# Four style-modulated convolutions as one: two start-up products move from VectorE to ScalarE, and two small pieces of work change places

## The reference

```python
for i, typ in enumerate(('same', 'upsample', 'same', 'downsample')):
    s = style @ mw[i].T + mb[i]                      # a scale per sample and input channel
    weight = SCALE * w[i] * s[:, None, :, None]
    demod = rsqrt(sum(weight * weight, axis=(2, 3)) + EPS)
    weight = weight * demod[:, :, None, None]        # 64 x 64 x 3, one per sample
    out = conv(out, weight) + b[i][None, :, None]    # 'upsample' and 'downsample' also blur with 1 3 3 1
return x + out
```

## Time and profile before

| | |
|---|---|
| median of 3 runs | 649.97 us (649.73 to 650.28) |
| the profiled execution | 650.42 us, its span 648.6 us |
| PE busy | 639.6 us, 99% of the span |
| DVE busy | 538.3 us, 83% |
| ACT, POOL busy | 387.0 and 388.9 us, 60% each |
| granted PE clock | 1.0 of full speed throughout |
| transfers | 125.05 MB, 193 GB/s on average |

### The profile page before, as it was taken

How to read it: one execution, slowest core, us unless ns; L and a number is a source line. 1 busy time by engine, 2 the same in 40 slices (tenths; PEclk the granted TensorE clock), 3 DMA queues, 4 the chain that set the end, 5 groups by cost and what they waited for, 6 DMA issues and landing times.

```text
span 648.6 us, 13049 instructions
## 1 busy us (share of the span) xinstructions
PE 639.6 (99%) x4756; PEld 613.6 (95%) x4756; DVE 538.3 (83%) x682; ACT 387.0 (60%) x752; POOL 388.9 (60%) x358
## 2 busy tenths in 40 slices
PE   9999999999999999999999999999999999999997
PEld 7799899999999999999999999999999999999987
DVE  5987988999898777789998987777989897787873
ACT  4776455765655766655766655666555666655552
POOL 3257477766566766467765666765657766557630
PEclk9999999999999999999999999999999999999999
DMA  8129888679877877986778878768977768987784
GB/s 264 38 72 255 212 189 205 158 199 228 208 169 193 207 205 200 222 202 158 184 198 219 206 180 215 193 180 209 232 169 191 186 185 220 225 211 179 182 202 162
DMA packets 145855, 125.05 MB, mean 193 GB/s; under 512 B 6080, under 2 KB 112512, under 8 KB 145792
## 3 DMA queue, kind: packets, MB, share of 16 engines
q1 hardware_dynamic: 145424, 123.97, 76.5%
q10 hardware_dynamic: 368, 0.25, 0.1%
HBM read 36.51 MB, written 33.75 MB: 108 GB/s over the span
## 4 chain that ended last, share of the span: by engine, by line
PE 90%; DVE 5%; ACT 2%; issue 1%; POOL 1%; DVEq 0%; ACTq 0%; POOLq 0%
PE po L203 14%; PE po L204 14%; PE po L205 14%; PE pg L203 8%; PE pg L205 8%; PE pg L204 8%; PE pm L205 5%; PE pm L204 5%; PE pm L203 5%; PE pg L208 4%; PE pg L209 4%; PE pe L460 1%; PE pg L469 1%; DVE T L868 1%; DVE W L920 0%
## 5 line engine op out<-in xcount | busy, mean ns | idle before, releaser
L203 PE MATMUL po<-xh,W 128*128 128x256 f32 (+1 forms) x640 | 199.9, 312 | 1.6 <-DVE T L868 1.2
L204 PE MATMUL po<-xl,W 128*128 128x256 f32 (+1 forms) x640 | 199.5, 312 | 0.0
L205 PE MATMUL po<-xh,W 128*128 128x256 f32 (+1 forms) x640 | 198.7, 311 | 0.0
L203 PEld LDWEIGHTS po<-xh,W 128*128 128x128 f32 x640 | 125.2, 196 | 7.4 <-issue 2.1
L205 PEld LDWEIGHTS po<-xh,W 128*128 128x128 f32 x640 | 125.4, 196 | 5.8
L204 PEld LDWEIGHTS po<-xl,W 128*128 128x128 f32 x640 | 126.0, 197 | 5.0
L859 DVE TENSOR_TENSOR xl<-X,xh 128x1290 fp32r<-128x1290 f32 (+1 forms) x64 | 126.3, 1974 | 4.9 <-ACT xh L573 3.9
L634 ACT CAST Gh<-Gf 128x512 fp32r<-128x512 f32 x64 | 39.5, 620 | 123.6 <-DVE Gf L890 123.6
L573 ACT CAST xh<-X 128x1290 fp32r<-128x1290 f32 (+1 forms) x64 | 87.6, 1369 | 18.3 <-PE po L205 14.7
L868 DVE SCALAR_TENSOR_TENSOR T<-po,DD,M 128x512 f32<-128x512 f32 x96 | 71.3, 743 | 31.3 <-ACT M L580 21.2
L580 ACT ACTIVATE M<-pm,cv,DD 128x256 f32<-128x256 f32 x96 | 54.0, 563 | 66.8 <-PE pm L205 65.8
(11 more groups left out here) (179 smaller groups left out, 1734.9 us busy)
## 6 DMA issues: line engine op xcount, KB each, us to landing
X<-in_xin SPq DMA_DIRECT2D x64, 516.0 KB, 4.5
out<-T SPq DMA_DIRECT2D x63, 512.0 KB, 5.8
W<-W SPq DMA_DIRECT2D x90, 256.0 KB, 4.3
W<-W SPq DMA_DIRECT2D x30, 384.0 KB, 5.6
V<-V SPq DMA_DIRECT2D x32, 256.0 KB, 5.0
V<-W SPq DMA_DIRECT2D x32, 128.0 KB, 4.4
V<-Vx SPq DMA_DIRECT2D x32, 128.0 KB, 4.0
W<-W SPq DMA_DIRECT2D x9, 128.0 KB, 3.0
```

The lines of the kernel that those rows point to most:

```text
L203: eng.matmul(o, wh_, rh, start=first, stop=False)
L204: eng.matmul(o, wh_, rl, start=False, stop=False)
L205: return eng.matmul(o, wl_, rh, start=False, stop=last)
```

## The change

1. tmp[:, 0] and tmp[:, 1] are made by two ACT activations (Copy, with the bias as scale), which wait for D10c and stand in ACT's queue in front of `high(0, 2)`; DVE's two instructions go. The factor 2 of the second moves into DVE's later update of tmp[:, 1], which becomes a scalar_tensor_tensor in the place of a tensor_tensor and waits for ACT's second product. PE's small matmul on tmp[:, 0] waits for ACT in the place of DVE.
2. The three products of `edges_begin` are made in the place of sample 4, in front of `x_low(3)`; `edge_in(0)`, which was their tail, stays in the place of sample 5.
3. In group NGR - 2 = 30, place 2 (sample 122), ACT makes `sums_high(31)`, the copies V and Vx of the last group's sums, ahead of `m_out(122)` and not behind it.

```diff
@@ -189,7 +189,7 @@
         s_wxh, s_wxl, s_x0h, s_x0l = sem("wxh"), sem("wxl"), sem("x0h"), sem("x0l")
 
 
-        SC_S, SC_SQ2, SC_A2, SC_S1, SC_D32, SC_A, SC_D10, SC_K1, SC_D, SC_K2, SC_K3, SC_CV = range(1, 13)
+        SC_S, SC_SQ2, SC_A2, SC_S1, SC_D32, SC_A, SC_D10, SC_D, SC_K2, SC_K3, SC_CV = range(1, 12)
 
         K_A2, K_B1, K_C, K_B1D = 1, 2, 3, 4
         def bc(ap, n):
@@ -541,7 +541,7 @@
             for x in PROLOGUE[7:]:
                 unit(*x)
             pe.wait_ge(s_in["ed"], 16)
-            pe.wait_ge(s_sc, SC_K1)
+            pe.wait_ge(s_ss, 4)
             for t in range(3):
                 m = pe.matmul(pe_[0:64, 0:128], E[0:64, 1, t, 0:64], tmp[0:64, 0, :], start=t == 0, stop=t == 2)
             m.then_inc(s_pp, 1)
@@ -673,6 +673,9 @@
             act.copy(B1dh[:], pb[1].rearrange("p (i h) o -> p i h o", h=2)).then_inc(s_k0, 1)
             q3_full(1)
             q3_high(1)
+            act.wait_ge(s_sc, SC_D10)
+            act.activation(tmp[:, 0], DD[:, 1], ACT.Copy, scale=BB[:, 0, 0:1]).then_inc(s_ss, 1)
+            act.activation(tmp[:, 1], S[:, P2], ACT.Copy, scale=BB[:, 0, 1:2]).then_inc(s_ss, 1)
             high(0, 2)
             high(0, 3)
             act.wait_ge(s_x[0], 16)
@@ -732,9 +735,9 @@
                         x_high(2 * g + 2)
                 elif i == 2:
                     highs(b, (4, 6))
-                    m_out(b)
                     if g == NGR - 2:
                         sums_behind(b - 1)
+                    m_out(b)
                     if g in (0, NGR - 2):
                         x_high(2 * g + 2)
                     sums_behind(b)
@@ -989,9 +992,6 @@
                 link(tt(b0z[:], AA[:, 0], DD[:, 0], ALU.mult))
                 tt(D10[:], DD[:, 0], DD[:, 1], ALU.mult)
                 link(dve.tensor_scalar(b0z[:], b0z[:], bias(0), None, ALU.mult))
-                dve.wait_ge(s_in["xe"], 16)
-                dve.wait_ge(s_ms, 2)
-                edge_in(0)
 
             def newton(l, t, step):
 
@@ -1056,8 +1056,6 @@
             reached(dve.scalar_tensor_tensor(out=D10c[:], in0=DD[:, 0], scalar=1.0 / 32.0, in1=DD[:, 1],
                                              op0=ALU.mult, op1=ALU.mult))
             dve.wait_ge(s_sc, SC_D10)
-            reached(dve.tensor_scalar(tmp[:, 0], DD[:, 1], bias(0), None, ALU.mult))
-            dve.tensor_scalar(tmp[:, 1], S[:, P2], bias(1), 2.0, ALU.mult, ALU.mult)
             full(0, 2)
             full(0, 3)
             g_low(0)
@@ -1074,7 +1072,9 @@
             sums(0)
             dve.wait_ge(s_pp, 5)
             link(tt(kt[lo], pe_[0:64, 0:128], D21[lo], ALU.mult))
-            reached(tt(tmp[lo, 1], tmp[lo, 1], kt[lo], ALU.add))
+            dve.wait_ge(s_ss, 5)
+            reached(dve.scalar_tensor_tensor(out=tmp[lo, 1], in0=tmp[lo, 1], scalar=2.0, in1=kt[lo],
+                                             op0=ALU.mult, op1=ALU.add))
             full(1, 0)
             full(1, 1)
             sums_low(0)
@@ -1103,12 +1103,16 @@
                     sums_low(weights_at(b - 1))
                 if i == 2 and g + 1 < NGR:
                     x_low(2 * g + 2)
+                if b == 4:
+                    edges_begin()
                 if b == 1:
                     x_low(1)
                 elif i == 0 and b:
                     x_low(2 * g + 1)
                 if b == 5:
-                    edges_begin()
+                    dve.wait_ge(s_in["xe"], 16)
+                    dve.wait_ge(s_ms, 2)
+                    edge_in(0)
                 for part, back in ((0, 1), (1, 2), (2, 6)):
                     if divmod(b - back, NG) in edge_at:
                         edge(*edge_at[divmod(b - back, NG)], part)
```

## The result

The changed kernel takes **647.17 us** (median of 5 runs, 646.56 to 647.62) against 649.97 (649.73 to 650.54): 2.80 us less, ratio 0.9955, 95% interval 0.994 to 0.997. The forecast was 647.0. The profiled execution took 647.62 us with a span of 645.8, against 650.42 and 648.6: also 2.8 less. So the two traces may be laid side by side, start by start.

What follows compares the result with a forecast made beforehand. PE, busy 99% of the span, was taken as the bound, so only its waits could pay: 0.35 + 0.66 + 1.05 + 0.40 + 0.2 + 3 x 0.1 = 2.96 us off 649.97 gave 647.0, range 646.3 to 648.8.

Steps and rivals of the forecast that it cites:

- the chain keeps most of it: Start-up, unit 4 to sample 0: most of Gl's 0.35 us gain lasts, ACT's copies being only 0.2 to 0.35 ahead.
- the lower bound: Start-up: only 0.2 us is gained if ACT's row of copies decides.
- the cover: Sample 4's place: DVE idled 2.53 us ahead of xl(3), so three products there delay nothing that PE shows.
- slow case: Sample 4's place: each product waits for a POOL instruction to end, all three done by about 58.25, xl(3) 0.1 later.
- rival a: Sample 4's place: products hold POOL up by 0.87 us, PE stands 0.6 us near 58, 647.6 us; chance 0.10.
- rival d: Sample 4's place: products delay POOL and with it PE's G product, so the kernel gets slower; chance 0.03.
- the gain: PE's waits for XS at the edges' first product, 0.66 us, and for T at sample 8, 1.05 of 1.14, go.
- slow restart: After a PE wait the second matmul also starts late, about 0.1 us, counted for three waits that go.
- rival c: Later groups: the wait returns at a group's first sample, taking back up to 2.0 us, 649.0 us; chance 0.15.
- rival b: Before sample 8: Vf, V low and xl(4) all blocked, T(6) 0.5 to 0.6 later, 647.6 us; chance 0.17.
- 0.40 + 0.2: Kernel's end: PE's wait before sample 123, 0.40 us, goes, and 0.2 of the 0.25 before sample 124.
- The rule about the shared ports: DVE instructions with two SBUF inputs contend with GpSimd's reads; whoever issues first keeps the ports for the whole instruction.

Runs made afterwards that it cites:

- e1: Kernel before with only the two constants' products moved to ACT: 650.02 us against 650.27, ratio 0.9995.
- e2: Kernel before with only the edges' three products moved to sample 4's place: 648.27 us against 650.27, ratio 0.9969.
- e3: Kernel before with only the last sums' copies put ahead of sample 122's M: 649.36 us against 650.27, ratio 0.9989.
- e5: Changed kernel with the edges' three products back in sample 5's place, but behind XS: 649.19 us, ratio 0.998 to the kernel before.
- e9: Changed kernel with the edges' three products made twice over in sample 4's place: 647.67 us, ratio 0.9963 to the kernel before.
- e6: Changed kernel with the edges' three products made three times over in sample 4's place: 648.17 us, ratio 0.9967 to the kernel before.
- e10: Changed kernel with the sums' copies ahead of M in the third place of every group, not only group 30: 646.29 us.

## Why the prediction was right, point by point

- **Part 1.** Forecast 0.35 us at Gl, bounds 0.2 to 0.4 at sample 0. Measured (changed kernel and e1): 0.38 and 0.37 at unit 4, 0.29 and 0.30 at sample 0. The step "the chain keeps most of it" lost 0.07 to 0.09, by the mechanism of the lower bound: ACT's copy of W (from 25.97) ends at 26.80 in both executions, so with the chance of 0.20 it gained 0.20 only, and DVE's low part of W behind it starts at 26.83, against 26.92 before, when DVE's own queue decided. The two ACT products cost nothing; they are issued 0.31 apart and overlap.
- **Part 2, the cover.** Forecast: slow case, products done at 58.25, xl(3) 0.1 later, nothing at PE. Measured: 58.17, 0.13, nothing. POOL was not held up (rival a): its two low parts took 0.79 and 0.74 us, against 0.74 and 0.73 before, and PE's products with G at 58 did not wait (rival d). POOL's room there is less than the 0.3 us that rival (a) counts, as a release takes 0.14 of it.
- **Part 2, the gain.** Forecast 0.66 + 1.05 and 0.1 for each slow restart, 1.91. Measured 1.88 at sample 8 and 2.00 to 2.02 at sample 9 (e2, and 2.11 - 0.09 in the changed kernel). The term that was off is T(6): forecast 73.8 on the time axis of the kernel before, measured 73.47 + 0.09 = 73.56. Vf lost only 0.24 (1.19 against 0.95) and not 0.6. XS lost 0.53 where 0.5 was forecast, but that is luck: the prediction had one of POOL's subtractions beside it, and it was Q3's low part, which had stood beside the first product before.
- **Given back (rival c), DVE not caught up (rival b).** e2 keeps its 1.9 us from sample 9 to the end. Both fall.
- **Part 3.** Forecast 0.40 + 0.2 + 0.1, bounds 0.4 to 0.8. Measured 0.79 and 0.78 (the changed kernel and e3). What the forecast lacked is the slow second matmul at sample 124 (0.09): it counts three such restarts in all, and there are four. M was not late: it starts at 625.58, and before at 627.58, with PE 2.00 ahead. The room for it, forecast as 0.6, does not hold if Vf is late: e5 shows that case.
- **The sum.** 2.96 forecast; by the ledger 0.29 (sample 0) + 0.67 (the edges' product) + 1.35 (sample 8 and the slow restarts, up to sample 9) + 0.79 (the end) = 3.10, less 0.20 of chance at start-up and 0.11 between samples 9 and 122, 2.79 in the profiled pair, and 2.80 in the medians. The forecast sum was thus 0.14 too small: 0.06 too much in part 1, 0.11 too little in part 2 and 0.09 in part 3, which partly cancel. That it agrees with the medians to 0.2 us is partly luck, since one comparison's medians can't tell 0.3 us (e1).
- **The rule about the shared ports** (the Trainium skill, page "SBUF — State Buffer", section "Who interferes with whom") has both its sides in these traces. With POOL first, DVE's products waited (1.20 us for one of 0.29). With DVE's xl first, POOL waited (2.32 us in e9). In e6 both lost: xl(3) waited for the POOL instruction in front of it, and POOL's next one waited for xl(3).

## What to carry to other kernels

When one engine is busy to 99%, list its waits one by one and price each as a difference of starts, the slow restart included; then a change to the work around it is worth what it removes from that list, and no more: the same reordering was worth 0.8 us in each of two places and nothing in 28 others, though it took some 22 us off VectorE's busy time there. Moving work into another engine's or place's idle time only pays if the queue behind it has room too: one place sooner gave 2.0 us, two places gave none, and three more products in the good place already cost 0.5 us through POOL, though VectorE itself had the time. Two waits in a row can be one: removing the first alone (e5) only moved its time into the second.

## What the runs showed of the hardware that was not expected

- A PE wait of 1.92 us was followed by 1.1 us of matmuls at the full clock and then, from 61.36 to 64.77, by matmuls 0.21 apart at the lower level (granted 0.83, 0.50 and 0.81 in three stretches of 2 us). Four of the twelve executions of that kernel, this one among them, have a mean clock of 0.997; the others have 0.999 to 1.0. A wait of 1.75 us in e5, and all of 0.98 and less, left the clock at 1.0 in the executions profiled. What decides between them stays open.
- A PE wait costs more than the idle time that the profile gives it: 0.15 to 0.17 us more between the starts of the last and the first matmul, and about 0.1 at the second matmul. The first part is how idle time is counted: a 256-column row ends 0.28 us after its start, but the next one could start after 0.12.
- Which of VectorE and POOL is issued first, by as little as 0.02 to 0.05 us, decides which of them is held up (e10: xl at 69.91, Gl at 69.93), and one change of order moved this in most groups of the kernel.
- Where several semaphores are waited for, the releaser in a trace can be the wrong one by 0.02 us (e6); the code settled it, and a second experiment agrees (e9, where the list names POOL).
